# Attention in a seamless rhythm of beats, with the residual added by an identity product on TensorE

## The reference

```python
x = x + attention(layernorm(x), ctx, ctx, mask)     # heads = 16, head_dim = 8
#   scores = Q K^T / sqrt(8), masked, softmax, times V, times Wo^T
h = layernorm(x)
logits = h @ wg.T                                   # 8 experts
w, idx = top_k(softmax(logits), 2); w = w / sum(w)
x = x + sum over the two experts e of  w_e * ((silu(h @ w1_e.T) * (h @ w3_e.T)) @ w2_e.T)
```

## Time and profile before

| | |
|---|---|
| median of 3 runs | 300.13 us (298.21 to 300.21) |
| profiled execution | 299.9 us, span of its instructions 298.1 us |
| mean granted TensorE clock | 0.825 of 2.4 GHz |
| TensorE busy | 218.6 us (73%) |
| VectorE busy | 210.4 us (71%) |
| ScalarE busy | 137.6 us (46%) |
| GpSimd busy | 104.1 us (35%) |

### The profile page before, as it was taken

How to read it: one execution, slowest core, us unless ns; L and a number is a source line. 1 busy time by engine, 2 the same in 40 slices (tenths; PEclk the granted TensorE clock), 3 DMA queues, 4 the chain that set the end, 5 groups by cost and what they waited for, 6 DMA issues and landing times.

```text
span 298.1 us, 5290 instructions
## 1 busy us (share of the span) xinstructions
PE 218.6 (73%) x1497; PEld 166.4 (56%) x1497; DVE 210.4 (71%) x622; ACT 137.6 (46%) x293; POOL 104.1 (35%) x116
## 2 busy tenths in 40 slices
PE   0786679888988979778587866198959999996010
PEld 0672547556774757655454543077848898875010
DVE  4659584866759576788497476748897788775095
ACT  5469396464564524525243543333434555553000
POOL 4356700020053001004516336501546654546740
PEclk9997599899797975988555965558999999999755
DMA  6932432412314041045310401140252322221537
GB/s 213 323 114 64 109 79 56 92 29 48 73 26 97 3 90 29 2 101 180 85 32 18 181 20 44 46 115 2 53 99 66 89 72 66 80 65 38 159 86 211
DMA packets 24793, 25.00 MB, mean 84 GB/s; under 512 B 3806, under 2 KB 19168, under 8 KB 24382
## 3 DMA queue, kind: packets, MB, share of 16 engines
q1 hardware_dynamic: 21502, 18.37, 24.5%
q0 software_dynamic: 2688, 5.48, 5.7%
q10 hardware_dynamic: 576, 0.82, 0.9%
HBM read 12.31 MB, written 6.31 MB: 62 GB/s over the span
## 4 chain that ended last, share of the span: by engine, by line
PE 38%; DVE 27%; DMA 13%; issue 9%; ACT 8%; POOL 3%; POOLq 1%; SPq 0%; DVEq 0%; ACTq 0%
PE bank L541 8%; DMA ys<-big 6%; DVE m_neg L1386 6%; PE bank L681 4%; PE bank L659 4%; PE bank L693 3%; DMA xg<-st_hi,rows_i 3%; PE bank L760 2%; ACT big L925 2%; POOL ys L1109 2%; DVE st L1371 2%; DVE rows L1162 2%; PE bank L763 2%; PE bank L761 2%; PE bank L786 2%
## 5 line engine op out<-in xcount | busy, mean ns | idle before, releaser
L1109 POOL DMA_INDIRECT ys<-big x39 | 38.0, 976 | 44.1 <-DVE big L1480 26.6
L925 ACT ACTIVATE big<-bank 128x512 f32<-128x512 f32 x64 | 36.5, 596 | 36.4 <-PE bank L693 35.6
L681 PE MATMUL bank<-bd,st 128*128 128x512 f32 x64 | 38.7, 612 | 12.5 <-DVE st L1371 6.7
L1386 DVE TENSOR_REDUCE m_neg<-bank 128x4 f32<-128x512 f32 x64 | 42.7, 684 | 6.4 <-PE bank L681 5.6
L1371 DVE SCALAR_TENSOR_TENSOR st<-st_hi,cst,bank 128x512 fp32r<-128x512 f32 x32 | 23.7, 747 | 26.4 <-ACT st_hi L916 24.4
L1070 POOL DMA_INDIRECT xg<-rows,rows_i x24 | 23.8, 994 | 41.1 <-DVE rows_i L1255 18.7
L827 ACT ACTIVATE st<-bank 128x128 fp32r<-128x128 f32 (+1 forms) x78 | 22.4, 329 | 24.6 <-PE bank L773 15.3
L693 PE MATMUL bank<-bd,st 128*128 128x512 f32 x64 | 31.9, 525 | 1.1 <-ACT big L925 1.0
L681 PEld LDWEIGHTS bank<-bd,st 128*128 128x128 f32 x64 | 15.5, 241 | 27.8 <-DVE m_neg L1386 17.3
L1039 POOL TENSOR_SCALAR ve<-mv 128x4 f32<-128x4 f32 x8 | 2.7, 332 | 79.0 <-DVE mv L1138 79.0
L786 PE MATMUL bank<-bd,st 128*128 x78 | 22.7, 312 | 9.3 <-DVE big L1480 9.2
(11 more groups left out here) (175 smaller groups left out, 534.8 us busy)
## 6 DMA issues: line engine op xcount, KB each, us to landing
bd<-st SPq DMA_DIRECT2D x62, 104.0 KB
big<-xg SPq DMA_DIRECT2D x39, 64.5 KB, 1.8
raw<-in_L_ffn_w SPq DMA_DIRECT2D x2, 1024.0 KB, 6.7
x_all<-in_x SPq DMA_DIRECT2D x4, 256.0 KB, 4.4
rows<-in_mask_BxS_if POOLq DMA_DIRECT2D x4, 256.0 KB, 4.7
ctx_all<-in_L_ffn_w SPq DMA_DIRECT2D x1, 1024.0 KB, 5.5
ctx_all<-in_ctx SPq DMA_DIRECT2D x3, 256.0 KB, 4.7
raw<-ys SPq DMA_DIRECT2D x3, 256.0 KB, 4.5
```

What stands on the lines that cost most here:

```text
L681: nc.tensor.matmul(s1[k % 2][:, :].rearrange("p (j q) -> p j q", j=NJ), st[:, p % 4, 0, b, g, :], bd_slot(1, 2 * p + b)[:, g, :, :], start ...
L925: nc.scalar.activation(prob[n % 2][:, NJ * g:NJ * (g + 1), :].rearrange("p h q -> p (h q)"), s2[k % 2][:, :], ACT.Exp, scale=SCALE).then_i ...
L1109: pool.indirect_dma_start(ys, bass.IndirectOffsetOnAxis(xt[n % XR][:, D:RW].bitcast(I32), 0), y_sb[n % YR], None, bounds_check=PAIRS - 1, ...
L1386: nc.vector.tensor_reduce(m_neg[:, H * b + g:H * (b + 1):NG], s1[k % 2][:, :].rearrange("p (j q) -> p j q", j=NJ), X, ALU.max, negate=True ...
```

## The change

The loop over passes has eight beats (`BEAT`) in each of eleven passes and no seam. Beat `t` of pass `p` holds the score by query `t` of pair `p`, and the score by key that lies 12 beats behind (`BEHIND`). Stack units stand one in a beat (`units`): the query units of the next pair in beats 2 and 3, the key units of the pair after it in beats 6 and 7; all use the work banks, and the scores' banks are used for scores only. The steps of a finished batch `n` come at fixed distances (`due`): values 17 beats behind beat `4n`, heads turned 18, normalised 19, turned back 20, copied 21, projected 22, taken 23. The quartets' steps, the weights' steps and the transposed maxima have new places in this rhythm.

The projection becomes two products into one bank, identity times tokens and heads times `Wo`, and ScalarE copies the sum over the tokens (`take_projection` moves from VectorE to ScalarE). The maxima are kept twice and rounded in two operations instead of three; their transpose gets a work bank instead of the bank of a score by key. Two of the eight clears of block diagonals move from ScalarE to GpSimd, and four stand in the first pass's beats. Six stack units are made ahead of the first score instead of eight.

On GpSimd the order of the inverse deviations (`inverse_deviation(m)`) follows the quartets' numbers.

```diff
-LEAD = 3
-TICKS = 2 * NG + LEAD
+BEAT = 2 * NG
+BEHIND = 12
...
+WEIGHT_STEPS = {(7, 0): [0], (7, 1): [1], (7, 2): [2], (7, 7): [3], (8, 4): [4], (8, 5): [5], (8, 6): [6], (9, 0): [7],
+                (10, 0): [8], (10, 1): [9], (10, 2): [10], (10, 3): [11]}
+LAST_STEP = NP + 2
...
+def units(p, t):
+    if t in (2, 3) and p + 1 < NP:
+        return [(p + 1, t)]
+    if t in (6, 7) and p + 2 < NP:
+        return [(p + 2, t - 6)]
+    return []
...
+def due(p, t, after):
+    n, rest = divmod(BEAT * p + t - after, NG)
+    return [n] if rest == 0 and 0 <= n < B else []
+
+FIRST_UNITS = [((0, 0), 0), ((0, 1), 1), ((0, 2), 2), ((0, 3), 3), ((1, 0), 6), ((1, 1), 7)]
...
@@ TensorE @@
             def project_out(n):
                 pe.wait_ge(onT_ready, n + 1)
...
-                nc.tensor.matmul(ob[n % 2][:, P:2 * P], onT[:, :], wo_s[:, :], start=True, stop=True).then_inc(y_full, 1)
+                nc.tensor.matmul(ob[n % 2][:, P:2 * P], ident, x_all[:, n, :], start=True, stop=False)
+                nc.tensor.matmul(ob[n % 2][:, P:2 * P], onT[:, :], wo_s[:, :], start=False, stop=True).then_inc(y_full, 1)
...
             def transpose_maxima(p):
                 pe.wait_ge(mhl_ready, p + 1)
-                if p >= 1:
-                    pe.wait_ge(prob_ready, 2 * NG * p - 1)
-                nc.tensor.transpose(s2[0][0:4 * H, 0:P], m_hl[:, :, :].rearrange("p a m -> p (a m)"), ident).then_inc(mt_full, 1)
+                transpose4(("MT", p), [m_hl[:, :, :].rearrange("p a m -> p (a m)")])
...
+            for p in range(LAST_STEP + 1):
+                for t in range(BEAT):
+                    tick = BEAT * p + t
+                    if p < NP:
                         scores_by_query(p, t)
+                    for n in due(p, t, 20):
+                        heads_by_dim(n)
+                    if 0 <= tick - BEHIND < NG * B:
+                        scores_by_key(*divmod(tick - BEHIND, BEAT))
+                    for n in due(p, t, 22):
+                        project_out(n)
+                    for unit in units(p, t):
+                        stack_unit(*unit)
                     for name in fills(p, t):
...
+                    for n in due(p, t, 17):
+                        values(n)
+                    for n in due(p, t, 18):
+                        heads_by_query(n)
...
@@ ScalarE @@
+            def take_projection(n):
+                act.wait_ge(y_full, n + 1)
+                copy(x_all[:, n, :], ob[n % 2][:, P:2 * P]).then_inc(x2_done, 1)
...
+                    for n in due(p, t, 18):
+                        take_heads(n)
+                    for n in due(p, t, 21):
+                        take_normalised(n)
+                    for n in due(p, t, 23):
+                        take_projection(n)
+                    if 0 <= tick - BEHIND < NG * B:
+                        probabilities(*divmod(tick - BEHIND, BEAT))
+                    for unit in units(p, t):
+                        stack_high(*unit)
+                    if (p, t) in ((0, 0), (0, 1), (0, 4), (0, 7)):
+                        clear_diagonal(QB + {0: 0, 1: 1, 4: 2, 7: 3}[t])
...
@@ GpSimd @@
             for u in range(1, NQ):
...
                 inverse_deviation(u)
                 context_rest(u)
-                if u == 2:
-                    inverse_deviation(NQ)
+            inverse_deviation(NQ)
+            send_quartet(0)
             inverse_deviation(NQ + 1)
-            send_quartet(0)
             inverse_deviation(NQ + 2)
             send_quartet(1)
             send_quartet(2)
...
@@ VectorE @@
-            def take_projection(n):
-                dve.wait_ge(y_full, n + 1)
-                nc.vector.tensor_tensor(x_all[:, n, :], ob[n % 2][:, P:2 * P], x_all[:, n, :], ALU.add).then_inc(x2_done, 1)
...
+                    if p < NP:
                         largest(p, t)
...
+                    for unit in (units(p, t - 1) if t else units(p - 1, BEAT - 1) if p else []):
+                        take_stacks(*unit)
+                    for n in due(p, t, 19):
+                        normalise_heads(n)
...
+                    if (p, t) in ((4, 5), (6, 5), (8, 5)):
+                        second_statistics((p - 4) // 2)
+                    if (p, t) in ((4, 7), (6, 7), (8, 6)):
+                        q = (p - 4) // 2
+                        normalise(QB * q, NQ + q)
...
+                    if (p, t) in ((6, 1), (8, 0)):
+                        place_rows((p - 6) // 2)
```

More of the change, by code:

```diff
@@ L147, in slot_order @@
-def slot_order():
[L149 to L154, removed]
-    slot, bank_of, turn, used = {}, {}, {}, {}
[L156 to L168, removed]
+BEAT = 2 * NG
@@ new lines, in fills @@
+def fills(p, t):
+    return ([("MT", p - 1)] if t == 1 and 1 <= p <= NP else []) + FILLS.get((p, t), [])
+def due(p, t, after):
+    n, rest = divmod(BEAT * p + t - after, NG)
+    return [n] if rest == 0 and 0 <= n < B else []
+FIRST_UNITS = [((0, 0), 0), ((0, 1), 1), ((0, 2), 2), ((0, 3), 3), ((1, 0), 6), ((1, 1), 7)]
+def slot_order():
+    order = [(("V", 0), 6), (("xT", 0), 7)] + [(("st", *unit), k) for unit, k in FIRST_UNITS]
+    for p in range(LAST_STEP + 1):
+        for t in range(BEAT):
+            order += [(("st", *unit), 6 + t % 2) for unit in units(p, t)]
+            order += [(name, 6 + t % 2) for name in fills(p, t)]
+    order += [(name, 7) for name in END_FILLS]
+    slot, bank_of, turn, used = {}, {}, {}, {}
+    for n, (name, k) in enumerate(order):
+        slot[name], bank_of[name], turn[name] = n, k, used.get(k, 0)
+        used[k] = used.get(k, 0) + 1
+    made = [name[1:] for name, _ in order if name[0] == "st"]
+    return slot, bank_of, turn, used, made
@@ L627, in stack_unit @@
                 o = claim(("st", p, k))
-                if k >= 2 and p >= 2:
-                    pe.wait_ge(max_done, 2 * NG * (p - 1))
                 if k == 0 and p == 0:
@@ L929, in _ @@
             tokens_high(0)
[L930 to L931 removed]
+            for unit, _ in FIRST_UNITS[:4]:
+                stack_high(*unit)
             take_values(0)
[L933 to L973 removed]
@@ L1079, in _ @@
             load_mask(1)
+            for k in (2, 3):
+                nc.gpsimd.memset(bd[:, k, :].bitcast(F32), 0.0).then_inc(more_cleared, 1)
+            own(nc.gpsimd.memset(va[1][:, :, :], 0.0))
+            v = va[1].rearrange("p (m i j) r -> p m i j r", i=2, j=NJ)
+            nc.gpsimd.memset(v[:, :, 0, :, 16:17], 1.0)
+            nc.gpsimd.memset(v[:, :, 1, :, 17:18], 1.0).then_inc(va_cleared[1], 1)
+            masks(1)
             stacks_in(pool, 0, 1)
@@ L1361, in take_stacks @@
                 is_k, h = UNITS[k]
-                n = 4 * p + k
+                n = made.index((p, k))
                 full(("st", p, k))
                 dve.wait_ge(sthi_ready, n + 1)
-                if k == 0 and p >= 4:
+                if k % 2 == 0 and p >= 4:
                     dve.wait_ge(s2_full, 2 * NG * (p - 3))
```

303 lines of the change are left out of this document (96 added, 207 removed), and 6 rows, old and new, of the table FILLS.

## The result

| | before | changed kernel |
|---|---|---|
| median of 4 runs each, us | 299.17 (297.46 to 300.21) | 308.39 (306.45 to 310.79) |
| ratio | | 1.032, 95% interval 1.022 to 1.042 |
| profiled execution, us | 299.9, span 298.1 | 310.8, span 309.0 |
| mean granted TensorE clock | 0.825 | 0.848 |

The change makes the kernel 3% slower; 282 was forecast.

The account below looks back on a forecast made before the run. It took the seams between passes, then GpSimd's scatters, to bound the kernel. Shorter passes and a shorter way to the first tile bring that tile 18.1 us earlier, at 174.1: span 280.0, forecast 282 us, range 268 to 297.

Parts of the forecast that it names:

- first maximum: Start: six stack units instead of eight ahead of the first score, so 22.2 us instead of 23.65.
- passes 0 and 1: ScalarE's clears and roundings bind pass 0 (11.2 us), VectorE binds pass 1 (9.7); both end at 43.1 instead of 54.85.
- passes 2 to 5: Without seams these four passes take 13.1, 13.1, 14.3 and 16 us: 56.5 instead of 74.2.
- pass 6, with the gap: VectorE waits 7.5 us before a normalisation for GpSimd's inverse deviation, now behind eight scatters; the pass takes 21.5 us.
- pass 7: No stack units; VectorE about 13 us, TensorE 17 at the lower clock or 9 at the higher; 15.5 taken.
- last maximum to third statistics: Third quartet's statistics, in beat 5 of pass 8, end some 6.5 us behind the last maximum, at 143.1.
- statistics to first tile: GpSimd's inverse deviation and scatters, then landing and issue: 31 us from third quartet's statistics to first tile, against 34.6.
- two further clears go to GpSimd: At the start, two more clears on GpSimd lie in its wait for the first stacks.
- that is 6.2 for four beats, 12.4 a pass: TensorE in passes 2 to 5: 5.5 us of work plus 0.7 wait per four beats; 13.1 a pass with fills.
- lower clock throughout: Rival: stack products spread over the beats no longer lift TensorE's clock; about 35 us more, 317 us; chance 0.09.
- Clock swings: Rival: TensorE's mean granted clock 0.75, passes 2 to 5 about 2.2 us longer each; 292 us; chance 0.15.
- tight coupling: Rival: beats pay each round trip, 2 us a pass more in six passes, longest stall; 296 to 300 us; chance 0.07.

Follow-up runs that it names:

- five mends: Changed kernel with late GpSimd clears, second quartet's deviation between scatters, statistics earlier, heads a beat later, tokens rounded at beat 5, two pass-0 edits: 280.83 us, ratio 0.939.
- early tokens alone: Changed kernel with ScalarE rounding the turned tokens at beat 5 of passes 0, 2 and 4, a beat earlier: 304.44 us, ratio to before 1.019.
- late clears alone: Changed kernel with GpSimd's diagonal clears behind its two diagonal transfers and the value buffer's clear behind the first quartet's context: 302.62 us, ratio to before 1.009.

## Why the prediction was wrong

The prediction's own terms, in us, against the profiled changed kernel and the five mends:

| step | forecast | changed | five mends |
|---|---|---|---|
| first maximum | 22.2 | 28.44 | 22.56 |
| passes 0 and 1 | 20.9 | 27.32 | 26.77 |
| passes 2 to 5 | 56.5 | 68.00 | 62.25 |
| pass 6, with the gap | 21.5 | 21.45 | 13.59 |
| pass 7 | 15.5 | 15.26 | 14.02 |
| last maximum to third statistics | 6.5 | 11.66 | 6.07 |
| statistics to first tile | 31 | 32.90 | 30.86 |
| first tile to the end | 105.9 | 103.97 | 101.98 |
| span | 280.0 | 309.0 | 278.1 |

The forecast of the first maximum started from 23.65, the cut of the earlier trace rows; the maximum itself starts at 24.16, so the same step from there gives 22.7. That is a small slip: with the clears moved, 22.53 was measured.

- **First failed step: "two further clears go to GpSimd, where they lie in the time in which it waits for the first stacks".** GpSimd's wait was there, but I asked only who was idle and not whom the clears would disturb. They cost 5.9 us at the first maximum; with them moved the kernel is 5.8 faster, to which the clock contributed. A normalisation on VectorE takes 0.33 us undisturbed and 6.0 when it meets the clears. The Trainium skill ("SBUF — State Buffer", "Who interferes with whom") says that a `tensor_scalar`, the normalisation's operation, can run in a two-port mode and then shares a pair of ports with GpSimd, which one of the two holds for a whole instruction while the other is fully blocked; an operation outside these modes with at most one input in SBUF does not contend. The rows agree with both: 6.0 us for the normalisation, and 0.75, the usual length, for the stacks, which take one tensor from SBUF and one from PSUM. In which mode an operation ran no row shows. I had not weighed this rule.
- **Second: "that is 6.2 for four beats, 12.4 a pass".** I counted one open round trip, through the normalised heads, at 0.7; it was 0.75 to 0.98 in seven of eight cases, 5.8 us in all where 5.6 was counted. So this term was right. I missed the second: the turned tokens of beat 5 fill a work bank that the stack unit of beat 7 needs, and ScalarE's rounding stood behind the unit of beat 6 (1.38 in passes 2 and 4, and 1.64 in pass 0). Of the 11.5 us by which passes 2 to 5 exceed the forecast, the tokens are 2.6 (passes 2 and 4 with the early rounding) and the clock 3.0; 5.9 was not taken apart. The heads one beat later take 2.0 off (passes 2 to 4, with pass 3 taken at equal clock), but off a wait that the forecast had.
- **Third: the statistics "some 6.5 us behind the last maximum".** 11.66, because a weight remainder that waits for ScalarE stood one beat ahead of them on VectorE. Moved, they come 7.9 behind it, and in the five mends 6.07. The order of one engine's rows was mis-read more than the length of the chain.
- **Passes 0 and 1** were costed by ScalarE's clears. They took 27.32, 6.4 over the forecast. TensorE in fact waited 3.54 us in pass 0 for the second quartet's normalised tokens, which wait for GpSimd, and 1.64 for turned tokens; at a mean granted clock of 0.69 and 0.83. The two passes take 24.25 with the early tokens alone, 29.58 with the late clears alone and 26.77 with all mends, still 5.9 over; where these come from stays open.
- **Right:** the gap of 7.5 us (7.63) and its cause; the length of pass 6, and of pass 7, whose 15.5 was a middle between two clock levels; the 31 us to the first tile, to 2; the identity product at nothing that can be measured; the seams' 24.4 us of waiting, which went.
- **Rivals.** The slower one (lower clock throughout) is not what happened: the mean granted clock in passes 2 to 5 is 0.92, against 0.86 before. Clock swings are there, worth 3 us in passes 2 to 5, not 10. The Trainium skill's rule on a matmul stream that idles at its PSUM banks ("TensorE: Matmul & The Clock Gate", "A second HAM failure mode: psum-queue depth-cycling") is not settled by this: pass 2 has 1.00 throughout although TensorE stands in it for 0.76, 0.48 and 1.38 us, and passes 3 to 5 have swings. Nearest was the tight coupling at 0.07, which I took to end at 296 to 300. None of my rivals was a delay that the change brings in at the start.

The five mends run in 280.8 us, near the forecast of 282, but that is luck and does not confirm the sum: their passes 0 to 5 take 11.6 us more than forecast, while pass 6, without the gap that I had counted in, and pass 7 take 9.4 less and the expert stage 3.9 less.

## What to carry to other kernels

Work that is moved to an idle engine is free only if it disturbs nobody: before moving a GpSimd operation, look at what VectorE does from SBUF to SBUF in the same microseconds. When a seam is taken out by spreading its work over beats, list for each engine what stands directly ahead of each operation that somebody waits for; every wait there, one beat too early, stops the whole rhythm. A change that comes out slower may still be right in its main part: here a few small moves of rows turned a loss of 3% into a gain of 6%.

## What the runs showed of the hardware

- VectorE's normalisation was held through three GpSimd clears in a row (6.0 us instead of 0.33) and did not get in between them; where GpSimd waited for the end of each clear before the next, it got in after one (2.5 us at most). Elsewhere two normalisations took 3.09 us beside a single clear of 1.8 us and ended with it.
- VectorE operations that read PSUM ran at their usual length beside the same clears (0.75 and 0.69).
- TensorE's spells at the lower clock level came in some of the profiled executions and not in others at the same place (pass 5: 17.5 us at 1.00, 19.4 at 0.87), worth 1 to 2 us each.
